# Content projections of eight heads at a time, unpacked by ScalarE into two groups' tiles

## The reference

```
B: kv_c = rms(x @ W_kv) * g_kv                     # rank 64
   q_c  = x @ W_q                                  # rank 128
   k = [heads(kv_c @ W_kdec, 16), rope(heads(x @ W_krope, 32))]
   q = [heads(q_c @ W_qdec, 16), rope(heads(q_c @ W_qrope, 32))]
   v = heads(kv_c @ W_vdec, 16)
   causal softmax(q k^T / sqrt(48)) v, then @ W_o
E: q, k, v = split(x @ Wqkv + bqkv)                # 16 heads of 16
   STRIDES = [1,1,2,2,2,2,4,4,4,4,8,8,8,8,16,16]   # head h uses every STRIDES[h]-th key
   softmax(q k[::stride]^T / 4) v[::stride], then @ Wout + bout
   layer norm, a 256-1024-256 network with ReLU, layer norm
```

## Time and profile before

| | |
|---|---|
| median of 3 runs | 3690.88 us |
| span of the profiled execution | 3688.1 us, 63212 instructions |
| PE busy | 3457.0 us (94%), 24928 matmul records |
| DVE busy | 2271.7 us (62%) |
| ACT busy | 1887.2 us (51%) |
| POOL busy | 955.1 us (26%) |
| mean granted TensorE clock | 0.965 of full speed |
| HBM read, written | 15.30 MB, 8.39 MB |

### The profile page before, as it was taken

One profiled execution on the slowest core, in us unless ns is written; L12 is line 12 of the kernel. 1 busy time (PEld: TensorE's weight loads), 2 busy tenths in 40 slices (PEclk: granted clock), 3 DMA queues, 4 the chain that ended last, 5 costly groups with the idle time before them and its releaser, 6 DMA issues.

```text
span 3688.1 us, 63212 instructions
## 1 busy us (share of the span) xinstructions
PE 3457.0 (94%) x24928; PEld 2002.6 (54%) x24928; DVE 2271.7 (62%) x4778; ACT 1887.2 (51%) x2919; POOL 955.1 (26%) x1069
## 2 busy tenths in 40 slices
PE   4789999999999999999999999999999999999876
PEld 3355556565555656555555655555565555555443
DVE  3446576666756666675666667566666756676442
ACT  2234655546465564646556464555646555564422
POOL 2213132331313232131222323122231313223111
PEclk8798999999999999999999999999999999999977
DMA  3000000000000000000000000000000000000000
GB/s 92 1 1 1 1 1 12 1 13 1 13 1 1 13 1 13 1 13 1 1 12 1 13 1 8 5 1 13 1 13 1 1 13 1 12 1 7 1 6 6
DMA packets 40882, 27.73 MB, mean 8 GB/s; under 512 B 19600, under 2 KB 39696, under 8 KB 40592
## 3 DMA queue, kind: packets, MB, share of 16 engines
q1 hardware_dynamic: 40592, 23.69, 2.2%
HBM read 15.30 MB, written 8.39 MB: 6 GB/s over the span
## 4 chain that ended last, share of the span: by engine, by line
PE 82%; DVE 12%; ACT 3%; issue 2%; POOL 0%; DVEq 0%; ACTq 0%; POOLq 0%
PE ps L478 74%; PE ps L489 8%; DVE MX L915 2%; DVE XN L843 1%; ACT other L1200 1%; DVE MX L909 1%; DVE XN L894 1%; DVE XN L891 1%; DVE XT L854 1%; DVE LT L881 1%; DVE XN L892 1%; DVE XT L853 1%; ACT PR L1174 0%; DVE stats L834 0%; DVE other L851 0%
## 5 line engine op out<-in xcount | busy, mean ns | idle before, releaser
L1174 ACT ACTIVATE PR<-ps 128x1024 f32<-128x1024 f32 (+3 forms) x592 | 524.5, 931 | 341.9 <-PE ps L478 340.6
L478 PE MATMUL ps<-MAT 32*128 32x512 f32 (+5 forms) x4928 | 593.3, 503 | 14.4 <-DVE MX L909 4.4
L915 DVE TENSOR_REDUCE MX<-ps 128x2 f32<-128x1024 f32 (+3 forms) x512 | 391.8, 818 | 203.7 <-PE ps L478 201.4
L1246 POOL TENSOR_TENSOR rstd<-var,neg_half 128x4 f32<-128x4 f32 x144 | 148.7, 1033 | 1311.3 <-DVE var L826 1183.5
L478 PEld LDWEIGHTS ps<-MAT 32*128 32x128 f32 (+2 forms) x4928 | 290.4, 199 | 262.4 <-issue 162.7
L478 PE MATMUL ps<-XT,cn_w 128*128 128x256 f32 x1536 | 367.6, 390 | 13.5 <-DVE XT L853 8.5
L478 PEld LDWEIGHTS ps<-XT,cn_w 128*128 128x128 f32 x1536 | 290.5, 193 | 99.7 <-issue 28.7
L478 PE MATMUL ps<-other,cn_w 128*128 128x512 f32 (+2 forms) x1152 | 321.0, 480 | 16.1 <-ACT other L1082 5.4
L921 DVE SCALAR_TENSOR_TENSOR MAT<-ps,MAT 128x512 f32<-128x512 f32 x128 | 88.5, 691 | 300.9 <-PE ps L489 300.3
L1281 POOL TENSOR_TENSOR MAT<-XN 128x512 f32<-128x512 f32 x128 | 167.3, 1307 | 402.4 <-DVE XN L894 241.8
L1304 POOL TENSOR_SCALAR_AFFINE_SELECT PR<-PR 128x512 f32<-128x512 f32 (+1 forms) x192 | 158.8, 827 | 410.0 <-ACT PR L1174 409.8
(11 more groups left out here) (158 smaller groups left out, 5718.2 us busy)
## 6 DMA issues: line engine op xcount, KB each, us to landing
X<-in_L_attn_x SPq DMA_DIRECT2D x16, 512.0 KB, 3.9
out<-X SPq DMA_DIRECT2D x16, 512.0 KB, 3.0
w_up<-in_L_attn_W SPq DMA_DIRECT2D x1, 1024.0 KB, 6.8
w_down<-in_L_attn_W SPq DMA_DIRECT2D x1, 1024.0 KB, 8.8
w_krope<-in_L_attn_W_krope SPq DMA_DIRECT2D x1, 512.0 KB, 4.4
w_qk<-in_L_attn_Wqkv SPq DMA_DIRECT2D x4, 128.0 KB, 4.4
cn_w<-in_L_ffn_cn_w SPq DMA_DIRECT2D x1, 256.0 KB, 4.2
w_qrope<-in_L_attn_W_qrope SPq DMA_DIRECT2D x1, 256.0 KB, 3.1
```

The costliest lines, as they stand in the source:

```text
L478: return pe.matmul(dst, lhsT, rhs, start=start, stop=stop, skip_group_check=True)
L915: last = dve.tensor_reduce(MX[:, t, at], src[:, :, a:a + nk[pair]], AX_X, ALU.max)
L1174: freed(act.activation(PR[0:m, tile_of((s, q, g, r)), 2 * pair:2 * pair + 2, lo:T], ps[0:m, b:b + 2, 0:T - lo], ACT.Exp, scale=SCALE[s]), ...
L1246: pool.tensor_tensor(rstd[:, c, :], var[:, c, :], neg_half[:], ALU.pow).then_inc(rstd_ready.sem, 1)
```

## The change

Content weights are no longer padded. A product now gives eight heads, two neighbouring groups, in 128 dense rows: in each stretch of 32 rows, 16 of a head of the even group (u = 0) and 16 of a head of the odd group (u = 1). The products are made at the step of the first group of a pair (`pair_of`: groups 0 and 2 in B, which runs upward, 3 and 1 in E, which runs downward); at the second group's step TensorE and ScalarE do nothing. In E the keys of a pair are computed with the smaller stride of the two.

ScalarE reads each product twice, and writes a whole tile of 128 rows for each group: scale is a column of zeros and ones (`c_keep`) that keeps the group's own rows, bias is the column with the row of ones (`c_one[u]`) or `c_qkb`. For u = 1 the row of ones is row 0 of a head instead of row 16, so MX has a second buffer, and the maxima of odd groups go to rows 0, 32, 64, 96. E's keys are taken from the product with a stride.

MAT has 12 tiles instead of 8: 4 for the rope halves and 8 for content, each with its own rotation, since a content tile is now written one group earlier. GpSimd's copy of the first group waits on a new semaphore (`first_content`), that of the second for the bank's release. The weights are loaded dense, in 28 DMAs in place of 7, without zeroing first, and the biases in 16 in place of 8.

The diff, cut to its core:

```diff
-MAT_TILES, HI_TILES = 8, 4
+ROPE_TILES, CONTENT_TILES, HI_TILES = 4, 8, 4
+MAT_TILES = ROPE_TILES + CONTENT_TILES
...
+def pair_of(s, g):
+    first, second = (2 * (g // 2), 2 * (g // 2) + 1)[::1 if s == "B" else -1]
+    return first, second
...
-        w_kdec = sb("w_kdec", [P, GROUPS, P])
+        w_kdec = sb("w_kdec", [P, 2, P])
...
-        MX = sb("MX", [P, TT, P])
+        MX = sb("MX", [P, 2, TT, P])
...
+        first_content = Signal("first_content", [(*st[1:4], w) for st in steps_of("content")
+                                                 if st[3] == pair_of(st[1], st[3])[0] for w in contents_in[st[1]]])
...
-                padded.append((dst.rearrange("p g (j r) -> p (g j) r", r=ROWS)[:, :, 0:HD],
-                               src.rearrange("k (h e) -> k h e", e=HD)))
+                columns = src.rearrange("k (f u j e) -> f u k j e", f=2, u=2, e=HD)
+                for f in range(2):
+                    for u in range(2):
+                        loads.append((dst[:, f, :].rearrange("p (j u e) -> p u j e", j=4, u=2)[:, u], columns[f][u]))
...
                 def content(s, q, g):
-                    c = q % CH
+                    if g != pair_of(s, g)[0]:
+                        return
+                    c, f = q % CH, g // 2
...
                     for w in "kq":
-                        step = STRIDES[4 * g] if w == "k" else 1
+                        step = STRIDES[8 * f] if w == "k" else 1
...
                 def contents(s, q, g):
-                    before = mat_before[s, q, g]
-                    if before:
-                        when_full(act, *last_exp(*before))
...
+                    for w in contents_in[s]:
+                        w = w[1]
+                        src = when_full(act, "content", s, q, f, w)
+                        for n, e in enumerate(pair_of(s, g)):
+                            before = content_before[s, q, e]
+                            if before:
+                                when_full(act, *last_exp(*before))
+                            u, at = e % 2, "qk".index(w) * GROUPS + e
+                            dst, keep = MAT[:, content_tile((s, q, e), w), :], c_keep[:, u:u + 1]
+                            if s == "E":
+                                step = STRIDES[4 * e] // STRIDES[8 * f] if w == "k" else 1
+                                cols_ = T // STRIDES[4 * e] if w == "k" else T
+                                last = act.activation(dst[:, 0:cols_], src[:, 0:cols_ * step:step], ACT.Identity, scale=keep,
+                                                      bias=c_qkb[:, at:at + 1])
+                            elif w == "q":
+                                last = act.activation(dst, src, ACT.Copy, scale=keep)
+                            else:
+                                b, _ = J["content", s, q, f, w]
+                                last = act.activation(dst.rearrange("p (v n) -> p v n", v=2), ps[:, b:b + 2, 0:T // 2],
+                                                      ACT.Identity, scale=keep, bias=c_one[:, u:u + 1])
+                            if n:
+                                freed(last, "content", s, q, f, w)
+                            else:
+                                last.then_inc(first_content.sem, 1)
...
                     for w in "qk" if s == "B" else "kq":
-                        read_out(pool, "content", s, q, g, w)
+                        if g == pair_of(s, g)[0]:
+                            pool.wait_ge(first_content.sem, first_content.at(s, q, g, "c" + w))
+                        else:
+                            read_out(pool, "content", s, q, g // 2, w)
```

More of the change, by code:

```diff
@@ L598, in content @@
                     for w in "kq":
-                        step = STRIDES[4 * g] if w == "k" else 1
-                        product(single_bank(), ("content", s, q, g, w),
-                                [(w_qk[:, f, "qk".index(w), g, :], XT[:, c, f, 0:T:step]) for f in range(KT)], cols_=T // step)
+                        step = STRIDES[8 * f] if w == "k" else 1
+                        product(single_bank(), ("content", s, q, f, w),
+                                [(w_qk[:, k, "qk".index(w), f, :], XT[:, c, k, 0:T:step]) for k in range(KT)], cols_=T // step)
                 def values(s, q):
@@ L914, in row_maxima @@
                                 a = first[pair]
[L915 removed]
+                                last = dve.tensor_reduce(MX[:, g % 2, t, at], src[:, :, a:a + nk[pair]], AX_X, ALU.max)
                         freed(last, "max", s, q, g, m, pair)
```

100 lines of the change are left out of this document (52 added, 48 removed).

## The result

The changed kernel takes 3736.5 us (median of four runs, 3735.1 to 3754.8) against 3690.7 for the kernel before. The medians are 1.2% apart; the ratio over all runs is 1.0134, with a 95% interval of 1.0112 to 1.0155, so the change is slower, and clear of noise. I had forecast 3660 and a range of 3600 to 3698, so both the size and the sign were wrong.

A forecast was written before the change was run, and what follows sets the result against it. TensorE was taken as bounding most of the path (82% of the chain), not everywhere. Terms -1.56 - 0.25 - 0.9 - 0.3 + 1.1 = -1.91 us a turn, times 16 = -31, gave 3660 us; range 3600 to 3698.

The forecast's parts named there:

- B.3: Content.B.3 removed: VectorE's work on G and maxima limit the gain to slack; -0.25 us a turn, between 0 and -1.1.
- E.2: Content.E.2 removed: it covered a wait for ScalarE's exponentials before exp.B.3.1; -0.9 us a turn, between -0.5 and -2.85.
- E.1 and E.0: Content.E.1 longer, +0.85; content.E.0 removed, GpSimd's bias earlier, mix faster, h1.A.1 earlier, -1.15; together -0.3 us a turn.
- B.0: Content.B.0: ScalarE's four bunched writes delay exp.E.0.3; +1.1 us a turn, between 0.6 and 1.3.
- B.1: Content.B.1 removed: nothing after it is late, so worth its whole length; -1.56 us a turn.
- rivals, 3 and 4: Clock falls once more a turn: smaller gain, 3684 (3674 to 3690), chance 0.19; or slower, 3715, chance 0.14.
- Rival 4: Clock fall as long as the present one meets dense matmuls at h1.A.1; +1.5 us a turn, 3715, milder 3700; chance 0.14.
- rival 1 and 2: TensorE bound in each place, 3555, chance 0.07; or half of it, E.2 and content.E.0 worth more, 3610, chance 0.15.
- At no cost: ScalarE's four writes at content.B.2, GpSimd's new wait and the second MX were to add no time to a turn.
- the cover: Slack at content.B.2: its pair of banks is asked for 5 us later, hiding the four writes; else up to 1.3 a turn.
- The loads: At the start, more and shorter DMAs; last issue some 10 us later, cost 0; without cover up to +5 once.

The follow-up runs named there:

- e1: Changed kernel plus seven dead products (512-column fp32, nobody reads) a turn: three at E.0, one at E.2, two ahead of sum.B.2.0, one ahead of exp.E.0.3; 3667.4 us.
- e9: Changed kernel with the two content products of B in the other order, keys before queries; 3683.0 us.
- e2: Changed kernel with three dead products a turn at E.0 alone, ahead of h1.A.1; 3683.9 us.
- e14: Changed kernel with two dead products a turn ahead of sum.B.2.0 alone; 3707.5 us.
- e13: Changed kernel with one dead product a turn ahead of exp.E.0.3 alone; 3736.6 us.
- e5: Changed kernel with dead products at E.2 (one), ahead of sum.B.2.0 (two) and ahead of exp.E.0.3 (one), none at E.0; 3696.8 us.
- e10: Changed kernel with keys before queries in B and dead products at E.0 (three), E.2 (one) and ahead of sum.B.2.0 (two); 3678.0 us.
- e4: Changed kernel with its own steps moved into the idles, including content.E.1 ahead of h1.A.1, no dead work; 3684.2 us.
- e17: Kernel before with one dead product a turn ahead of content.E.2; 3718.9 us.
- e7: Changed kernel with the dense pair in B alone; in E each group has its own products again; 3695.8 us.
- e18: Changed kernel with own steps moved into the idles, exp.E.3.0 moved behind proj.B, and three dead products a turn at B.3 and E.2; 3626.7 us.

## Why the prediction was wrong

Point by point. The offset of a step from its turn's start is compared between the kernel before (turn at 736.7), after (745.0) and e1 (735.8, without a fall).

| term of the sum | forecast | after, one fall | e1, no fall |
|---|---|---|---|
| B.3 | -0.25 | -0.20 | -0.25 |
| E.2 | -0.9 | -0.97 | -0.97 |
| E.1 and E.0 | -0.3 | +1.21 | -0.25 |
| B.0 | +1.1 | +1.27 | +1.36 |
| B.1 | -1.56 | -1.64 | -1.64 |

**The local terms were right.** With the clock at full all five are within 0.3 us (e1's dead products stand in the waits and leave the steps behind them where they are); with one fall, four are. Their sum of -1.91 stands against -1.7 (214.8 to 213.1) in a fall-free turn. The working behind them held too: exp.B.3.1 waits 0.87 for ACT PR; max.B.3.1 is freed by VectorE 0.28 after it asks; exp.E.0.3 waits 0.88 for ScalarE's last content write.

**E.1 and E.0: right in each mechanism, wrong in one number.** GpSimd's bias came early, the mix's operations ran in 0.42 each, and h1.A.1 started on VectorE's word, as forecast. But I let its 16 records take 3.5 us; in after they take 5.17, since the clock fell there. That is the missing 1.5. The Trainium skill (SBUF — State Buffer, "Who interferes with whom") states the port pair shared by VectorE and GpSimd as an exclusive lock; the 0.42 with the bias out of the way, against 1.48 beside it, agrees.

**The clock is the step that failed.** The sum had no term for the clock, which put it at nothing, and left it to two rivals, 3 and 4. Rival 4 named the mechanism and a point from which it decides, 3.8 us at half clock a turn; measured were 13.4 a turn after against 3.4 before, 10.0 more. The result of 3736.5 lies beyond even its 3700 to 3715, because both rivals counted one new fall, at E.0. The waits at B.3, E.2 and B.0 stand in the same text, and were priced only as waits. In nine of the thirteen middle turns the clock falls four times: right behind the idles at B.3, E.0 and B.0, and once at 58 to 60, ahead of the idle at E.2, which no term or rival had. I gave these two rivals a third of the chance, and ended the range at 3698, just below rival 4. The Trainium skill (TensorE: Matmul & The Clock Gate, "A second HAM failure mode: psum-queue depth-cycling") says that frequent short idles at bank waits make the clock swing and cost throughput; the trace of after agrees for three of the four falls, with 174 us at half for 44, and not for the one at 58 to 60.

**Against rival 1 and 2.** The idles at the four places, together 6.9 us a turn against 0.6 before, show that TensorE was not the bound there: of 8.5 us of removed work some 6.3 came back as waits, and a fall-free turn gained 1.7.

**At no cost.** Content.B.2's writes cost nothing in after; e9 showed the cover by taking it away, 0.86 a turn. The loads cost nothing: the last issue came at 61.71, 12 us later, and VectorE's first use of w_kdec at 74.57, 0.9 later:

```profile
61.71 1.43 SPq L1412 DMA_DIRECT2D X<-in_L_attn_x  x1
...
74.57 0.35 DVE L1049 TENSOR_SCALAR w_kdec<-w_kdec,cols 128x256 f32<-128x256 f32 x1
```

**What stays open.** That the loss is the clock's is shown by equal records at two clocks in one trace and by e1. That it falls because TensorE idles more is borne out for three places, each filled alone: E.0 in e2, B.3 in e14, B.0 in e13, and in each the falls right behind that idle are gone. Most of the falls at 55 to 60 are not explained by it: they come ahead of the idle at E.2, and in e1, e5 and e10 without one. What brings them in after, at 58 to 60 in nine turns, is open. e4, e9 and e17 show besides that the length of an idle doesn't settle whether a fall comes, and no run here could set idle and kind of work apart from the turns before.

## What to carry to other kernels

Work that is taken from a nearly always busy TensorE is worth its length only where nothing else is late, and every wait that takes its place can have a second price: count the new idles of a turn, and give each a possible fall of the clock, beside its length. Look for turns or loop passes of one trace with equal records and different lengths before any other comparison; they give the price of the clock without an experiment. When dense work leaves a hole, move own dense work into it, and try one dead product to see quickly whether the hole or its clock is what costs.

## What the runs showed of the hardware

- Equal records took 203.26 or 211.05 us of PE time in two turns of one execution, with 3.4 and 20.5 us at half clock. I had not expected the same program to swing so much from turn to turn.
- Seven dead products a turn, 6.5 us of work, made a kernel 69 us faster (3736.5 to 3667.4); one dead product a turn in the kernel before made it 27 us slower, 13 more than its length.
- One program's runs scattered from 3680 to 3704 us (e7) with the mean clock between 0.965 and 0.956, and another's from 3671.8 to 3698.5 (e4, 0.944 to 0.935), while a third's five runs stayed within 0.5 us (e18).
- Falls also came in stretches in which TensorE didn't idle at all, among small products (e17 at 56, the kernel before at the same place), and in the changed kernel one was over before the idle beside it began (1465.06, where the idle of 1.01 us ends at 1466.77).
